# Recurrent layer with a mixture of experts on one core: GpSimd's transfers paced by the transposed state, scatters spread over more steps

## What is computed

```python
xn = layernorm(x)
s = attn(xn)                      # state-space layer
g = silu(ffn(xn))                 # mixture of 8 experts, the best 2 per token
out = x + s * g

# attn: a scan over 512 positions, state of 64 per sequence
def step(state, bc):
    b_t, c_t = bc
    s = layernorm(state @ A_bar + b_t, ln_st_g, ln_st_b)
    return s, c_t * s

# ffn: for each token the two experts with the largest logits
topw, topi = top_k(logits, 2)
w_dense = sum(one_hot(topi) * softmax(topw))
h = gelu(xn @ ew1 + eb1)
moe_out = (h @ ew2 + eb2) weighted by w_dense, then three rotations
```

## Time and profile before

| | us |
|---|---|
| median of 3 plain executions | 393.1 |
| lowest, highest | 390.68, 395.04 |
| profiled execution: span from first to last instruction | 440.3 |
| of it: TensorE busy | 347.8 (79%) |
| VectorE busy | 284.8 (65%) |
| ScalarE busy | 191.5 (44%) |
| GpSimd busy | 162.5 (37%) |

### The profile page before, as it was taken

The page is one execution under the profiler, slowest core; times in us unless marked ns, Lnnn a source line. Parts: engine busy times, 40 slices in busy tenths (PEclk is TensorE's granted clock), DMA queues, the critical chain, the costliest instruction groups (busy, mean ns, idle before and its releaser), DMA issues.

```text
span 440.3 us, 11604 instructions
## 1 busy us (share of the span) xinstructions
PE 347.8 (79%) x4014; PEld 261.9 (59%) x4014; DVE 284.8 (65%) x1320; ACT 191.5 (44%) x563; POOL 162.5 (37%) x225
## 2 busy tenths in 40 slices
PE   1869979867886778777877889978888979779872
PEld 1758956664453446666656667756666654556541
DVE  3886349993564555664655555566888865688873
ACT  1235863200221224454544555664767644874220
POOL 7060000166666555655564444432545540000000
PEclk9996976857586868998898899996999998999795
DMA  8389920004112213654454456693566415001002
GB/s 267 65 192 180 170 32 1 3 30 177 44 42 64 72 44 104 213 167 164 148 181 159 154 178 220 205 363 115 186 203 204 167 60 183 19 39 37 24 26 78
DMA packets 44157, 54.80 MB, mean 124 GB/s; under 512 B 6840, under 2 KB 28767, under 8 KB 44095
## 3 DMA queue, kind: packets, MB, share of 16 engines
q1 hardware_dynamic: 38975, 42.52, 33.5%
q0 software_dynamic: 4544, 9.39, 6.6%
q10 hardware_dynamic: 576, 2.10, 1.4%
HBM read 14.15 MB, written 16.63 MB: 70 GB/s over the span
## 4 chain that ended last, share of the span: by engine, by line
PE 57%; DVE 21%; issue 10%; ACT 4%; another core or an unknown queue 3%; DMA 3%; SPq 1%; DVEq 0%; ACTq 0%
PE bank L1086 16%; PE bank L1527 8%; PE bank L1537 6%; DVE wT L987 3%; PE bank L1426 2%; DVE ring L999 2%; PE bank L1557 2%; PE bank L412 2%; PE bank L1497 2%; PE bank L459 2%; PE bank L419 2%; DMA record<-experts 2%; PE bank L1520 1%; PE bank L1505 1%
## 5 line engine op out<-in xcount | busy, mean ns | idle before, releaser
L1748 POOL DMA_INDIRECT token_rows<-rows_out,token_rows_i x78 | 75.5, 968 | 93.4 <-PE bank L1086 63.1
L1086 PE MATMUL bank<-Mrep,wT 32*32 32x64 f32 x2368 | 69.5, 236 | 46.1 <-DVE wT L987 30.5
L1086 PEld LDWEIGHTS bank<-Mrep,wT 32*32 32x32 f32 x2368 | 46.2, 113 | 91.4 <-issue 90.6
L999 DVE SCALAR_TENSOR_TENSOR ring<-bank,Rho,Dv 128x64 f32<-128x64 f32 x112 | 31.7, 283 | 74.3 <-PE bank L1086 55.1
L1734 POOL DMA_INDIRECT sorted_rows<-late,slots x64 | 62.7, 979 | 46.1 <-PE bank L1086 20.5
L1652 ACT ACTIVATE desk<-bank,record 128x128 f32<-128x128 f32 x156 | 48.9, 365 | 63.2 <-PE bank L1527 56.0
L1527 PE MATMUL bank<-desk,record 128*128 128x128 f32 x312 | 59.1, 315 | 0.7 <-DMA record<-experts 0.7
L1537 PE MATMUL bank<-record,desk 128*128 128x129 f32 x312 | 50.6, 287 | 0.0
L1527 PEld LDWEIGHTS bank<-desk,record 128*128 128x128 f32 x312 | 43.5, 202 | 8.6 <-issue 1.5
L1537 PEld LDWEIGHTS bank<-record,desk 128*128 128x128 f32 x312 | 43.7, 203 | 0.1
L1644 ACT ACTIVATE desk<-bank,cols 128x128 f32<-128x128 f32 x78 | 35.9, 460 | 4.0 <-PE bank L1520 4.0
(11 more groups left out here) (333 smaller groups left out, 652.7 us busy)
## 6 DMA issues: line engine op xcount, KB each, us to landing
record<-experts SPq DMA_DIRECT2D x78, 290.5 KB
sorted_rows<-zero_rows SPq DMA_DIRECT2D x2, 2515.5 KB, 28.1
desk<-sorted_rows SPq DMA_DIRECT2D x26, 193.5 KB
pulls<-token_rows SPq DMA_DIRECT2D x8, 516.0 KB, 5.1
X<-in_L_attn_x ACTq DMA_DIRECT2D x4, 512.0 KB, 6.2
out<-xT SPq DMA_DIRECT2D x8, 256.0 KB, 2.2
token_rows<-rows_out,token_rows_i POOLq DMA_INDIRECT x78
experts<-in_L_ffn_ew SPq DMA_DIRECT2D x1, 1024.0 KB, 6.4
```

The source lines that it names most:

```text
L999: dve.scalar_tensor_tensor(out=state(r, k), in0=psY, scalar=Rho[:, k:k + 1], in1=Dv[:, k, :], op0=ALU.mult, op1=ALU.add).then_inc(sem("sta ...
L1086: t = pe.matmul(psY[q], wT[q, 32 * c:32 * c + 32], Mrep[q, c, :], start=(c == 0), stop=(c == 1))
L1748: pool.indirect_dma_start(token_rows[h], bass.IndirectOffsetOnAxis(ap=token_rows_i[:, g:g + 1], axis=0), rows_out[:, g % OUT_PLACES, :], N ...
```

## The change

In rounds 0 and 1 (`r < MAGIC_ROUNDS`, steps 0 to 51) GpSimd's waits ahead of a scatter and ahead of a transfer of finished rows are for `state_T` with the step's `turn`, no longer for `product`. From step 52 they are for `product` as before. The table of scatters becomes one per step in steps 0 to 23, and in steps 24 to 58 one per step except where t - 24 is a multiple of five. The first half's last scatter (number 31) then belongs to step 19, the last of all to step 58. Nothing else changes.

```diff
-        SCATTERS_AT = {t: (2, 1, 2, 1, 2)[t % 5] for t in range(20)}
-        SCATTERS_AT.update({t: 1 for t in range(20, 25)})
-        SCATTERS_AT.update({t: 1 for t in range(25, 55) if t % 2 == 0})
+        SCATTERS_AT = {t: 1 for t in range(24)}
+        SCATTERS_AT.update({t: 1 for t in range(24, 59) if (t - 24) % 5})
         assert SCATTER_LEAD + sum(SCATTERS_AT.values()) == 4 * Q
...
                 for t in range(STEPS):
                     r, k, turn = round_of(t)
                     j = SLOT_AT.get(t - 1)
+                    paced = sem("state_T") if r < MAGIC_ROUNDS else sem("product")
                     if j is not None and 3 <= j:
-                        pool.wait_ge(sem("product"), turn)
+                        pool.wait_ge(paced, turn)
                         rows_back(j - 3)
                     for _ in range(SCATTERS_AT.get(t, 0)):
-                        pool.wait_ge(sem("product"), turn)
+                        pool.wait_ge(paced, turn)
                         scatter(sent)
                         sent += 1
```

## The result

The changed kernel is slower. Its median is 407.66 us in four executions (401.74 to 411.99) against 394.07 in four of the kernel before (390.68 to 396.55). The ratio is 1.0283, with an interval of 1.0205 to 1.0361; like every ratio here it takes only the fast executions (401.74 and 406.38 against 390.68, 393.1 and 395.04), without those more than 1.5% above the fastest of their kernel. The forecast was 397.2, in a range of 382 to 404. Each ratio further down is to executions of the kernel before that were taken along with that run.

A forecast was written before the change was run, and what follows sets the result against it. It took the 148-step scan chain (add, transpose, product) as the bound, with late adds mostly an artefact of profiling. 391.2 without them, plus 4.1 (0.1 + 2.8 + 1.2) and 1.9 around it, gave 397.2 us, range 382 to 404.

The forecast's parts named there:

- Its direction: Whole kernel: slower 0.40, same 0.36, faster 0.24.
- Holds belong to the profiled execution: Scan: adds later than both inputs allow, 49.1 us over 148 steps, mostly in the profiled execution and hardly in plain runs.
- the faster: Rival, first round: late adds also occur in plain runs, and removing two-transfer steps gains time: 383.5 us; chance 0.22.
- the much slower one: Rival, rounds 0 and 1: late adds are real and state_T puts each on its own product: 401.5, up to 409; chance 0.13.
- The last sign of being wrong: Scan: adds following products by 0.14 us although transfers run would show the prediction wrong.
- State_T: Rounds 0 and 1: transfers start 0.73 to 1.4 us after the add; nobody in the scan waits, cost 0.
- The first half's loads: Scatter 31 moves from step 12 to 19; first sorted rows land 0.1 us late, bounds 0 and 3.
- GpSimd's rate: Steps 24 to 58: 57 transfers at 1.26 us plus row numbers take 73.8 us, 10.3 behind; 2.8 reaches the scan.
- Rival 1: Steps 24 to 58: transfers cost less than 1.26 us or places give more slack; nothing shows, 393.1 to 395; chance 0.20.
- the second half's loads: Scatter 63 moves from step 54 to 58; its rows land 1.2 us late for step 66, bounds 0 and 3.5.
- the slack of the output places: ScalarE's copy into output places tolerates GpSimd being 7.5 us behind; the excess, 2.8 us, is pushed into the scan.
- What waits for the load: Step 66: slot 39's transpose wants the rows 11.5 us after add 58; they land at 12.75.

The follow-up runs named there:

- before again: The kernel before, unchanged, profiled once more: span 389.5 us, time 391.37 us.
- the four other kernels of the table: Changed kernel with waits on product throughout, six output places, row numbers three slots earlier, or those last two together: ratios to before 1.0323, 1.0285, 1.0294, 1.0301.
- a sixth place: Changed kernel with six output places in place of five: 405.34 us, ratio 1.0285 to the kernel before.
- earlier numbers: Changed kernel with each chunk's row numbers added up three slots earlier: 406.39 us, ratio 1.0294 to the kernel before.
- the 22 spaced scatters: Changed kernel with 30 scatters in steps 0 to 23 and 22 in two of three steps from 24 to 57: 399.95 us, ratio 1.0128 to before.
- the table alone: Changed kernel's new scatter table, all waits on product as in the kernel before: 405.91 us, ratio 1.0323 to before.

## Why the prediction was wrong

Its direction had the largest of the three chances, and its mechanism, GpSimd pushed beyond its rate in steps 24 to 58, is what happened. The size was short: 4.1 us in the sum, 9.6 in the traces up to step 69, and more than that in the median, which lies above the range.

- *Holds belong to the profiled execution:* right, shown by before again. With it fall the rivals that took them as real, the faster and the much slower one. The last sign of being wrong, adds that follow the products by 0.14 although transfers run, was set the wrong way round: before again shows it (in steps 52 to 83 the median is 0.15 us), and it bears out the sum, which is made without holds.
- *State_T:* 0 predicted, nothing measured (1.0025). In the first round scatters start 0.84 us after the add, within 0.73 to 1.4.
- *The first half's loads:* 0.1 late predicted. The rows of the changed kernel's timeline that answer to the earlier trace rows, scatter 31 first:

```profile
137.41 0.95 POOL L1733 DMA_INDIRECT sorted_rows<-late,slots  x1 [0.81 <-DVE wT L987]
...
139.70 1.45 SPq L1791 DMA_DIRECT2D desk<-sorted_rows  x3
...
142.38 0.35 PE L1519 MATMUL bank<-ident,desk 128*128 128x128 f32 x1 [0.64 <-DMA desk<-sorted_rows]
```

  SP is through 2.68 us before the transpose (about 3 predicted), which waits 0.64 us for the rows. Step 20 takes 3.68 us in both kernels, so it costs nothing.
- *GpSimd's rate:* 57 transfers with their row numbers were put at 73.8 us, or 72.5 from the first start to the last. The first starts at 150.19 and scatter 63 at 222.66: 72.5. By the Trainium skill (Perfetto Trace Analysis, section "GPSIMD Engine Instruction"), start-to-start spacing counts and not the span; the trace agrees, with 72.47 / 56 = 1.29 us against spans of 0.96. Rival 1, plain transfers that cost less, is out.
- *The step that failed* is "the second half's loads", put at 1.2 us, by way of the backlog that it starts from, "GpSimd 7.5 behind" at add 58. The backlog measured 12.2 (222.66 against add 58 at 210.50). Steps 59 to 69, for which the sum has only the 1.2, lost 7.3: 5.2 up to add 65 and 2.1 behind it. Three things made it so. First, I let GpSimd start the 57 at add 23; it starts 3.3 us after it (146.91), where it had waited 3.14 us for the first finished row's copy. Second, I took 63.5 us for these 35 steps from the disturbed execution less its holds; the unhindered scan takes 61.3. So the backlog is 3.3 + 73.8 - 61.3 = 15.8 us and not 10.3. Third, I cut it at the slack of the output places, as though all beyond 7.5 were passed to the scan by step 58. Only 2.3 were (2.8 predicted); 5.2 more came in steps 59 to 65 (1.8 of it at the lower clock), where I had no crowding at all, because the finished rows still stand behind the scatters.
- *What waits for the load:* I counted the rows alone, wanted in step 66, at 11.5 us after add 58. Before again has slot 39's transpose at 221.52, 13.1 after it, and in no trace does it wait for the rows. The record of tile 36 is wanted a step sooner and stands behind the load in SP's list. The prediction did not name what is queued behind that wait.

With these in place the sum comes out for the profiled execution: scatter 63 at 3.3 + 72.5 = 75.8 us after add 23, layer 1 of slot 38 6.1 later at 81.9. In before again it is 219.36 - 147.12 = 72.2 after. That is 9.7 us late, in whichever wait it is paid, and 9.6 were measured. On top of before again's 391.37 it makes 401.1, and the changed kernel's profiled execution took 401.74. That is the shortest of the four. The others took 406.38, 408.94 and 411.99, at a mean granted clock of 0.895, 0.875 and 0.876 in place of 0.909, and have no trace. What may add to the loss in them is seen in the four other kernels of the table with the same late date: from layer 1 of slot 38 to add 69 they take 2.3 to 4.5 us longer than the changed kernel's profile, at a granted clock of 0.55 to 0.72. My sum has no term for that. That it is the same in the executions without a trace is not shown.

## What to carry to other kernels

A backlog on an engine off the critical path is priced by a date: start plus count times spacing gives when its last item is done, and from there the chain to whoever needs it, everything queued behind the waiting instruction included. Waits ahead of that date and the wait at it are the same microseconds, so taking one of them away (a sixth place, earlier numbers) gained nothing here while the date stood. The date is a lower bound and not the whole price: the 22 spaced scatters waited past theirs, and a stall can be followed by a lower clock. And a single profile whose span is a tenth above the plain times is to be taken again before durations are read from it.

## What the runs showed that I had not expected

One profiled execution can be longer by 50 us than its repeat, with holds behind nearly every transfer that no other trace here has; not even the stretch without the holds could be used as it was (63.5 us against 61.3). What held the adds there is not shown.

TensorE's granted clock fell around the waits in most of these profiles, as the last column of the table has it. The changed kernel's layer 1 took 0.71 us after its wait of 2.20, at full clock. With early numbers it waited 5.23 us, and the same four matmuls took 1.23. In the 22-scatter kernel a wait of 2.35 us was followed by 1.22. The changed kernel had such a fall too, sooner: from 217.7 to 221.1, behind a wait of 2.64 us for ScalarE that ended at 217.5, its granted clock was 0.50. The longest is that of the table alone; its busy times from layer 1 to add 69:

```profile
229.71:241.00 11.29, 11.29 (x104) 9.26 (x105) 3.25 (x18) 4.17 (x13) 4.28 (x6) 0.55 0.58 190
```

Of the 22-scatter kernel two such rows, from add 65 to add 66 and from there to add 69:

```profile
219.50:224.83 5.33, 3.13 (x27) 2.65 (x28) 1.11 (x6) 1.84 (x6) 3.64 (x5) 0.68 0.76 243
224.83:232.95 8.12, 8.12 (x79) 6.56 (x80) 3.25 (x18) 2.92 (x9) 2.15 (x3) 0.58 0.35 116
```

At a granted clock of 0.58, most of the time then at the lower level of 1.2 GHz, steps 67 to 69 take 8.12 us; before again does them in 226.17 - 221.19 = 4.98 at full clock. So a stall of a few us of TensorE can be followed by 3.1 us more of loss (4.5 in the table alone), and much the same wait (2.20 in the changed kernel) by none. These are single executions; what makes the clock fall in one and not in the other is not shown.
